# One core, one layer stack: the last batch's attention values computed during the first scan, with paired scan products and weights rounded once

## The reference

```
xc   = silu(causal_conv(in_proj @ ctx.T))          # 512 channels, 4 taps
B, C, dt = x_proj @ xc ; delta = softplus(dt_proj @ dt + b)
state_t  = state_{t-1} * exp(delta_t * A_n) + delta_t * u_t * B_t[n]     # n = 0..15
y_t      = sum_n state_t * C_t[n] ; y = (y + D*u) * silu(layernorm(x).T)
x = x + y.T
x = x + bitlinear(gelu(bitlinear(layernorm(x), w1)), w2)
    # weight_quant: clip(round(w / mean|w|), -1, 1), one mean for each row of w
x = x + softmax(rms(q) @ rms(k).T / sqrt(128)) @ v @ Wo   # 16 heads of 128; k = ctx@Wk, v = ctx@Wv
out = x + mixture of 8 experts (top 2, bf16) + one shared expert
```

## Time and profile before

| | |
|---|---|
| median of three runs | 1864.55 us |
| the profiled execution | 1868.66 us, its span 1867.0 us |
| TensorE busy | 1773.8 us (95%), 8314 products |
| TensorE weight loads | 1133.9 us (61%) |
| VectorE, ScalarE, GpSimd busy | 1206.2, 1087.6 and 261.7 us |
| mean granted TensorE clock | 0.983 |
| first scan | about 48 to 220 us |
| attention groups of the last turn | 1382 to 1653 us |

### The profile page before, as it was taken

One profiled execution on the slowest core, in us unless ns is written; L12 is line 12 of the kernel. 1 busy time (PEld: TensorE's weight loads), 2 busy tenths in 40 slices (PEclk: granted clock), 3 DMA queues, 4 the chain that ended last, 5 costly groups with the idle time before them and its releaser, 6 DMA issues.

```text
span 1867.0 us, 26032 instructions
## 1 busy us (share of the span) xinstructions
PE 1773.8 (95%) x8314; PEld 1133.9 (61%) x8346; DVE 1206.2 (65%) x1549; ACT 1087.6 (58%) x2450; POOL 261.7 (14%) x250
## 2 busy tenths in 40 slices
PE   8899999999999999999999999999889999988898
PEld 4455545767765476766645676775457767644453
DVE  6999778977875798777678977776452010124542
ACT  5767457766754775666557766664555555445350
POOL 0002111000101010000101100010031101105570
PEclk9999999999999999999999999999999999999999
DMA  7355312323231122323122222323134332402535
GB/s 227 102 170 161 110 42 68 97 80 106 77 86 63 56 99 85 90 79 95 64 81 74 82 85 86 95 79 118 46 130 85 80 77 67 95 15 82 142 118 180
DMA packets 112891, 176.03 MB, mean 94 GB/s; under 512 B 11936, under 2 KB 64416, under 8 KB 112304
## 3 DMA queue, kind: packets, MB, share of 16 engines
q1 hardware_dynamic: 97776, 157.20, 27.4%
q0 software_dynamic: 14224, 16.28, 4.1%
q10 hardware_dynamic: 816, 1.57, 0.3%
HBM read 146.29 MB, written 35.02 MB: 97 GB/s over the span
## 4 chain that ended last, share of the span: by engine, by line
PE 79%; DVE 9%; ACT 6%; issue 4%; POOL 1%; DMA 0%; ACTq 0%; DVEq 0%; SPq 0%; POOLq 0%
PE ps L1980 27%; PE pp L1980 18%; PE px L1980 17%; PE pd L1980 6%; PE po L1980 5%; DVE arena L1516 3%; DVE arena L1508 2%; PE pp L2336 1%; ACT hbuf L1277 1%; PE pd L2307 1%; PE po L2307 1%; POOL xg_dram L903 1%; DVE arena L1527 1%; DVE fsc L1680 1%; PE ps L2176 1%
## 5 line engine op out<-in xcount | busy, mean ns | idle before, releaser
L1516 DVE TENSOR_TENSOR_SCAN arena<-arena 128x512 f32<-128x512 f32 x256 | 292.2, 1203 | 4.2 <-ACT arena L1016 3.6
L1277 ACT ACTIVATE hbuf<-ps,shift,rms_k 128x512 f32<-128x512 f32 x256 | 198.6, 777 | 123.1 <-PE ps L1980 115.6
L1980 PE MATMUL ps<-qkT_rows 128*128 128x512 f32 x512 | 250.7, 601 | 6.7 <-ACT hbuf L1277 2.8
L1980 PE MATMUL pp<-wq,xnT 128*128 128x256 f32 x1024 | 236.7, 386 | 2.9 <-issue 2.2
L1980 PEld LDWEIGHTS pp<-wq,xnT 128*128 128x128 f32 x1024 | 193.8, 194 | 29.1 <-ACT xnT L1232 4.3
L831 POOL TENSOR_TENSOR rms<-ssv,minus_half 128x4 f32<-128x4 f32 x64 | 82.0, 1281 | 863.6 <-ACT ssv L1253 863.6
L1016 ACT ACTIVATE arena<-arena,a_neg 128x512 f32<-128x512 f32 x256 | 163.7, 722 | 0.0
L1980 PEld LDWEIGHTS po<-v_ext,hbuf 128*128 128x128 f32 x768 | 105.9, 191 | 61.2 <-issue 61.2
L1980 PEld LDWEIGHTS ps<-qkT_rows 128*128 128x128 f32 x512 | 82.2, 190 | 83.6 <-ACT hbuf L1277 58.2
L1508 DVE TENSOR_TENSOR arena<-arena,bc 128x2048 f32<-128x2048 f32 x56 | 126.3, 2287 | 6.7 <-issue 5.6
L1735 DVE TENSOR_TENSOR xc<-xc,px 128x512 f32<-128x512 f32 x64 | 43.4, 678 | 134.3 <-PE px L1980 134.3
(11 more groups left out here) (339 smaller groups left out, 3002.8 us busy)
## 6 DMA issues: line engine op xcount, KB each, us to landing
bc<-bc_dram SPq DMA_DIRECT2D x56, 512.0 KB, 5.5
wo<-in_Wo SPq DMA_DIRECT2D x32, 512.0 KB, 3.6
wq<-in_Wq SPq DMA_DIRECT2D x32, 512.0 KB, 3.6
qkT_rows<-kt_dram SPq DMA_DIRECT2D x32, 512.0 KB, 4.5
hbuf<-in_w SPq DMA_DIRECT2D x8, 1024.0 KB, 9.6
wv<-in_Wv SPq DMA_DIRECT2D x32, 256.0 KB, 2.9
wk<-in_Wk SPq DMA_DIRECT2D x25, 256.0 KB, 3.1
kt_dram<-xnT SPq DMA_DIRECT2D x12, 512.0 KB, 2.6
```

What stands on the lines that cost most here:

```text
L1277: nc.scalar.activation(pT[:, h, k], ps[s_use % 2][:], ACT.Exp, bias=shift[:, 0:1], scale=rms_k[:, bass.ds(G * (GH * NT) + (h * NT + k), 1) ...
L1516: V.tensor_tensor_scan(hb[i][:, e], dA[i][:, e], hb[i][:, e], 0.0, ALU.mult, ALU.add).then_inc(scan_done[i], 1)
L1980: return nc.tensor.matmul(out, lhsT, rhs, start=first, stop=last, **kw)
```

## The change

It has four parts.

**Values.** The values of batch 3 are no longer made in the groups of the last turn. A table `WORK` gives each round of the first scan its items, key units (K) and value units (V): rounds 0 to 3 hold K2, K3-4, K5-6 and K7-9, round 4 V0-4, round 5 V5-7 and K10, round 6 K11-13, round 7 K14-15. A value unit is sixteen 128x256 products into `pp`, two copies on ScalarE and a 512 KB store to the new `v_dram`; its weights come into `wv` and `wk` by turns. In the last turn SyncE loads `v_sb` from `v_dram` (`v_load`) once the group before has made its last product with it. The context of batch 3 is loaded behind unit K9, and that of batch 0 behind V7.

**Pairs.** In rounds 3 to 6 (`PAIRED`) VectorE adds the products of the two states (`pair_c`), and TensorE adds the sum to y in one step (`y_pair`, behind the item `PAIR_BEHIND`) where two stood.

**Weights.** VectorE writes `w * w_inv + MAGIC_16` in float32 once; its upper half holds the rounded weight plus a constant. TensorE turns that half by one product with the identity in place of two, and ScalarE takes the sign with `minus_bits` as bias (Sign, int16 source) where it copied.

**SyncE.** In each round only the first item's loads and store stand ahead of the loads of B and C; those of the others stand behind.

```
+WORK = [
+         [("K", 2)],
+         [("K", 3), ("K", 4)],
+         [("K", 5), ("K", 6)],
+         [("K", 7), ("K", 8), ("K", 9)],
+         [("V", 0), ("V", 1), ("V", 2), ("V", 3), ("V", 4)],
+         [("V", 5), ("V", 6), ("V", 7), ("K", 10)],
+         [("K", 11), ("K", 12), ("K", 13)],
+         [("K", 14), ("K", 15)],
+]
+PAIRED = (3, 4, 5, 6)
...
@@ SyncE
+            def v_dma(m):
+                sp.wait_ge(pp_full[1], v_at(m))
+                if m + 2 < NG:
+                    wv_ahead(m + 2)
+                elif m % 2 == 0:
+                    w_load("v", 0)
+                else:
+                    w_load("k", first_unit(KEYS_BEFORE[m])[1])
+                    ctx_load(0)
+                for j in range(2):
+                    sp.wait_ge(pp_drained[j], v_at(m) + 1)
+                sp.dma_start(v_dram[m], v_stage_first[V_STAGE[m]]).then_inc(k_stored[V_STAGE[m]], 16)
...
@@ SyncE
             for r in range(TC):
-                for n in round_units(r):
-                    first_dma(n)
+                front_dma(*WORK[r][0])
                 if r + 2 < TC:
...
+                for kind, n in WORK[r][1:]:
+                    front_dma(kind, n)
...
+                        if b == V_BATCH:
+                            bank, n = d_at(turn_, g, GH - 1)
+                            sp.wait_ge(px_full[bank], n)
+                            v_load(g + 1)
...
-                    nc.scalar.activation(dst, src, ACT.Copy).then_inc(px_drained[bank], 1)
+                    nc.scalar.activation(dst, src, ACT.Sign, bias=minus_bits[:, 0:1]).then_inc(px_drained[bank], 1)
...
@@ ScalarE
+                for at_, (kind, n) in enumerate(WORK[r]):
+                    if kind == "K":
+                        first_out(n)
+                    else:
+                        first_v_out(n)
+                    for i in range(GH):
+                        if at_ == 0 and r + 1 < TC and not r == i == 0:
+                            decay(0, r + 1, i)
+                        if at_ == 1 and r + 2 < TC:
+                            tern(w_out, r + 2, range(2 * i, 2 * i + 2))
+                        if kind == "K":
+                            first_sums_out(n, i)
...
-                    V.tensor_scalar(w_plus[i][:, at], stage[i][:, at], w_inv[:, i, k:k + 1], 0.5, ALU.mult, ALU.is_gt).then_inc(signs_done, 1)
-                    V.tensor_scalar(w_minus[i][:, at], stage[i][:, at], w_inv[:, i, k:k + 1], -0.5, ALU.mult, ALU.is_lt).then_inc(signs_done, 1)
...
+                    V.tensor_scalar(w_round[i][part_][:, at % (HID // 2):at % (HID // 2) + half], stage[i][:, at:at + half], w_inv[:, i, k:k + 1],
+                                    MAGIC_16, ALU.mult, ALU.add).then_inc(signs_done, 1)
...
@@ VectorE
+            def pair_c(r):
+                for i in range(GH):
+                    dve.wait_ge(hc_done[i], r + 2)
+                V.tensor_tensor(hc_first[0], hc_first[0], hc_first[1], ALU.add).then_inc(hc_paired, 1)
...
@@ TensorE
+            def y_pair(r):
+                pe.wait_ge(hc_paired, PAIRED.index(r) + 1)
+                for e in range(EC):
+                    m = mm(y_first[e][:], ident[:], hc_first[0][:, e], False, True, skip_group_check=True)
+                m.then_inc(y_added, GH)
...
-                        mm(out, w_plus[i][:, at:at + P], ident_bf[:], True, False)
-                        m = mm(out, w_minus[i][:, at:at + P], minus_bf[:], False, True)
+                        m = mm(px[bank][:, k * P:(k + 1) * P], w_bits[i][part_][:, at:at + P], ident_bf[:], True, True)
...
@@ TensorE, group
-                        v_rows(0)
-                        v_rows(1)
+                        if b != V_BATCH:
+                            v_rows(0)
+                            v_rows(1)
```

More of the change, by code:

```diff
@@ L101 @@
 U_FIRST = G_FIRST * (B - 1)
+V_BATCH = 3
+WORK = [
[9 more added lines that the diff above has]
+PAIRED = (3, 4, 5, 6)
+PAIR_BEHIND = {r: max([1] + [i for i, item in enumerate(WORK[r]) if item == ("V", NG - 1)]) for r in PAIRED}
+ITEMS = [("K", 0), ("K", 1)] + [item for items in WORK for item in items]
+assert [n for kind, n in ITEMS if kind == "K"] == list(range(U_FIRST + 1)) and [n for kind, n in ITEMS if kind == "V"] == list(range(NG))
+KEYS_BEFORE = [sum(kind == "K" for kind, _ in ITEMS[:ITEMS.index(("V", m))]) for m in range(NG)]
+VALUES_BEFORE = [sum(kind == "V" for kind, _ in ITEMS[:ITEMS.index(("K", n))]) for n in range(U_FIRST + 1)]
+V_STAGE = [(k + KEYS_BEFORE[:m].count(k)) % 2 for m, k in enumerate(KEYS_BEFORE)]
+CTX_FRONT = B if V_BATCH == B - 1 else B - 1
 K_OFF = {"KT": 0, "SS": 2}
@@ L363, in program @@
         hq_step = sem("hq_step")
-        f_tmp = sem("f_tmp")
         x2_done = sem("x2_done")
@@ L523, in first_unit, with ctx_after @@
             return n, G_FIRST if n == U_FIRST else FIRST_BATCHES[n // G_FIRST] * NG + n % G_FIRST
+        def ctx_after(n):
+            return V_BATCH if V_BATCH == B - 1 and n == KEYS_BEFORE[0] - 1 else FIRST_BATCHES[n // G_FIRST + 1]
         def stored_by(end, parity):
-            return 16 * ((end + 1 - parity) // 2)
+            return 16 * ((end + 1 - parity) // 2 + V_STAGE[:values_before(end - 1)].count(parity))
         U_EARLY = 2
[L530 to L535, removed]
         def for_batches(turn):
@@ L1086, in first_sums_out, with first_v_out @@
                 k_sums_out(*first_unit(n), 0, h)
+            def first_v_out(m):
+                stage_ = V_STAGE[m]
+                act.wait_ge(k_stored[stage_], 16 * ((KEYS_BEFORE[m] + 1 - stage_) // 2 + V_STAGE[:m].count(stage_)))
+                for j in range(2):
+                    act.wait_ge(pp_full[j], v_at(m))
+                    nc.scalar.activation(v_stage_first[stage_][:, 2 * j:2 * j + 2], pp[j][:].rearrange("p (t h d) -> p t h d", t=2, h=GH),
+                                         ACT.Copy).then_inc(pp_drained[j], 1)
             def ctx_load(s):
@@ L1505, in times_b @@
                     dve.wait_ge(hc_done[i], g + 1)
+                elif s is FIRST_SCAN and g - 1 in PAIRED:
+                    dve.wait_ge(hc_paired, PAIRED.index(g - 1) + 1)
                 else:
@@ L2330, in v_rows, with v_drained @@
                         m.then_inc(v_full[j], 1)
+                    def v_drained():
+                        for j in range(2):
+                            pe.wait_ge(v_out[j], v_turn(G) + 1)
                     def q_turned(h):
@@ L2351, in values @@
                     def values(h, k):
-                        for j in range(2):
-                            pe.wait_ge(v_out[j], G + 1)
+                        if b == V_BATCH:
+                            pe.wait_ge(v_in, g * 16 + 16)
+                        else:
+                            v_drained()
                         pe.wait_ge(ones_set, b + 1)
```

172 lines of the change are left out of this document (103 added, 69 removed).

## The result

The changed kernel takes 1874.99 us in the median of 14 runs (1867.46 to 1880.51); the kernel before, on the same chip, 1865.50 (1863.38 to 1868.00). The ratio is 1.0046, 95% interval 1.0036 to 1.0056: some 9 us slower. Predicted were 1858 us and a range of 1840 to 1868. The profiled execution of after took 1871.52 us (span 1869.9), 2.9 more than the one of before. It is the fourth fastest of the 14, and the one of before is slower than all 14 beside it, so the two profiles show 2.9 of some 9 us.

What follows compares the result with a forecast made beforehand. VectorE was taken to set the first scan's rounds with TensorE close behind, TensorE alone to bound the last turn. Terms -26.6 + 13.6 + 4.9 + 1.7 = -6.4 us gave a median of 1858 us, range 1840 to 1868.

Steps and rivals of the forecast that it cites:

- the clock term: TensorE's spells at low clock behind waits, 1.7 us each: none to four possible (0 to 6.8), one taken, +1.7 us.
- Rounds of the first scan: TensorE's list with its waits in the first scan: y at 234.1 against 220.5, +13.6 us.
- The waits, taken as 19: TensorE's waits in the first scan for banks, contexts, turned weights, squares and key weights: 19 us in all.
- The last key unit: Unit 15 moves behind round 7's sums, so the next scan's products start 10.6 us behind y, not 5.7: +4.9 us.
- Values out of the last turn: Removing value products saves 3.62 us in each of seven last-turn groups and 1.25 in the first: -26.6 us.
- At nothing: Items given no cost of their own: the turned weights' second product (counted elsewhere), ScalarE's sign, SyncE's new order.
- The savings on VectorE: Halved weight conversions in the first scan and ahead of it save VectorE 8.4 us, against 10.0 for the pairs' additions.
- Half the waits: Low end of the forecast's own spread: only half of TensorE's first-scan waits occur, giving 1846 us.
- three more spells of 1.7: High end of the forecast's spread, 1867 us: three more low-clock spells, or first-scan waits half as much again.
- TensorE has the room: Rival for the first scan: TensorE takes up the waits and VectorE sets the rounds; -22.7, 1842 us, chance 0.16.
- The value units starve: Rival for the first scan: value weights land in 6 us, six units wait 2.8 each; +10.4, 1875 us, chance 0.14.
- The "slower" side: Whole-kernel outcome above 1868.3 us: chance 0.16, of which the forecast itself gave 0.02.

Runs made afterwards that it cites:

- run 1: The changed kernel with products of no effect put into TensorE's waits; 1866.68 us, ratio 0.9981 to the kernel before.
- run 2: The changed kernel without the pairs, so TensorE makes four more sums; 1891.55 us, ratio 1.0126 to the kernel before.
- run 7: The changed kernel with ScalarE reading sums before decays in rounds 3 and 6, round 7's weights turned behind V7; 1877.27 us, ratio 1.0050.
- run 12: The changed kernel with half of the values' products in the first scan left out (output wrong); 1868.64 us, ratio 1.0012 to the kernel before.
- run 5: Only the weights and SyncE parts of the change, with products of no effect in TensorE's waits; 1864.99 us, ratio 0.9978 to the kernel before.
- run 3: Only the weights and SyncE parts of the change, values in the last turn, no pairs; 1872.63 us, ratio 1.0020 to the kernel before.
- run 8: Only the weights and SyncE parts of the change, each identity product issued twice; 1863.78 us, ratio 0.9981 to the kernel before.
- run 11: The changed kernel with identity products issued twice and added products of no effect in TensorE's waits; 1867.67 us, ratio 1.0012 to the kernel before.
- run 4: The weights, SyncE and pairs parts of the change, values still in the last turn; 1870.17 us, ratio 1.0011 to the kernel before.
- run 10: Only the weights and SyncE parts, identity products issued twice, plus products of no effect in TensorE's waits; 1860.53 us, ratio 0.9968 to the kernel before.
- run 6: The kernel before with products of no effect put into TensorE's waits; 1869.14 us, ratio 1.0002 to the kernel before unfilled.
- run 9: The changed kernel with added products of no effect cut nearer to the waits' length, 183 in the first scan; 1873.94 us, ratio 1.0031.

## Why the prediction was wrong

**The step that failed is the clock term**, "+1.7, one spell, bounds 0 to 6.8". It measured 9.8 us in the profile: 7.3 in the rounds up to y, and 2.5 in the first group of the last turn, against 1.7 and outside its own bounds. The rest of the sum nearly stands. For the profiled execution I predicted -6.4, and it was +2.9:

- *Rounds of the first scan, +13.6 to y.* Round 3 started at 108.04 (107.9 predicted). From there to y were 133.6 us where 126.2 were laid out: 7.4 more, and the four slow units in it are 7.3 over the full clock. The waits, taken as 19, were about right as a total: TensorE's idle time in the list is 15.4, and some 18 with the 0.17 us by which the end of a product overlaps the next one when there is no wait. One by one they were not: K8 and K12 waited 1.6 each for 3.6 and 3.4, the contexts 1.5 and 2.0 for 2.3 and 1.3, and the turned weights 1.1 in round 2 and 2.9 in round 5, for 1.5 and 4.4.
- *The last key unit, +4.9.* From y to the next scan's products 10.5 us (10.6 predicted), +4.9: right.
- *Values out of the last turn, -26.6.* A group gave 3.45 for 3.62, since 0.17 of the 3.62 lay under the next product's start: 24.2. The first group gives 1.27 with the wait filled (run 1; 1.25 predicted), but cost 1.2 us. Of these 2.5, 1.4 go with the low clock behind its 3.31 us wait, since runs 2, 7 and 12 have that part alone; 1.1 come from the stretch ahead of the group, which they do not have. So -23.0.
- *Between and behind*, where nothing was predicted: +2.2 from the first turn to the last, -2.0 behind the groups. Their low stretches lie differently in the two profiles. The part behind the groups differs by up to 6 us between profiles in which it is the same code (run 5), so I take both numbers for chance; this is not shown.

I had the right row and a fair price of one spell (1.7 predicted, 1.0 to 2.9 measured), and counted waits of over a microsecond as four, though my own list gives five. The error was to take one spell for the likeliest: five came in the first scan. And two of them stand behind waits of 1.1 us which before had as 0.9 without any harm. The halved products that lengthen these waits stand in the prediction under "At nothing", as a saving counted elsewhere; run 3 against run 8 shows 7 us on exactly that edit.

How much of the 9 us the clock costs is less well shown than that it costs. The 7.3 are lengths of units in one profile. Filling the waits brought the median down by 12 us (run 1), yet y by 2 in the profile, and in run 11, with the clock up, by nothing, since the added products take their own time. The median missed by more than the profile, too: -6.4 predicted, +9.5 measured. Of that the median of after is 3.5 us above its own profiled execution, which goes with its clock (0.972 for 0.974), and that of before 3.2 below its own, which no run here explains.

Three sums of the prediction are off in themselves. The savings on VectorE add up to 8.6, not 8.4. Half the waits would give 1848.5 and not 1846. And three more spells of 1.7 make 1863, not the 1867 beside which they stand.

**The rivals.** "TensorE has the room" is refuted by runs 2 and 4: four sums cost TensorE's full time, and eight value units most of it. "The value units starve" gave the right number, 1875, by luck: the values' loads landed in 3.2 and 3.9 us, not in 6, and no unit waited for them. The "slower" side that came true had no rival of its own.

**Was the change sound apart from the clock?** With the waits filled it is no better than its smallest part, the weights: 0.9981 and 1.0012 (runs 1 and 11) against 0.9978, 0.9981 and 0.9968 for the weights alone (runs 5, 8 and 10). The ledger says why: the last turn gives 25.4 us (run 1, from the start of its first group to the end of its last), and 29.3 are lost up to the first turn (run 4 against after, the clock low in both, the move of the last key unit among it).

Not settled: SyncE's order was in every one of these kernels and was never tried alone; pairs without values were run only at the low clock; no run takes the clock's effect away without adding work on TensorE; and what exactly brings a low stretch is open.

The Trainium skill, TensorE: Matmul & The Clock Gate (A second HAM failure mode: psum-queue depth-cycling), describes a kernel whose TensorE idles for very short times between groups of products, so often that its clock goes back and forth between the two levels. These traces agree in that: the waits in front of the slow units are 1 to 3 us in a kernel that is 95% busy, and the clock fell and rose five times between 97 and 195 us.

## What to carry to other kernels

Work removed from TensorE next to a short wait can make the kernel slower: look at the granted clock in windows of one round, not at its mean over the span, and ask of each edit whether it widens a wait or thins the work beside one. Where the profile shows slow stretches behind waits, products of no effect ahead of the waiting instruction are a quick test of what the clock takes: they cost nothing where they only fill waits off the path (run 6), and their full time where TensorE is the bound and they overshoot (run 11). Before moving work into another stage, total what the bound engine has idle there. TensorE had 1.4 us of 21 in a round, some 7 in five rounds, and the pairs freed 14; eight units of 3.6 us could not fit.

## What the runs showed that was not expected

- 0.2 us more wait and 0.9 us less work in each round (runs 3 and 8) decided between a clock of 0.88 and 0.98 over 117 us.
- Some 15 added products fewer, of 198, keep only a quarter of the gain: after 1.0046, run 9 1.0031, run 1 0.9981.
- Taking 13 us of products out brought 6 us, and the mean clock did not rise with it: 0.970 (run 12), 0.972 in after.
- The two widest spreads of runs belong to kernels with slow stretches, after over 13 us and run 12 over 14, run 10 over 5. But run 3, with such stretches in five rounds, spreads over 6, less than the 7 to 8 of the kernel before beside the later runs.
